# Dealing a two-term combination to three engines instead of one, in an attention plus mixture-of-experts kernel

## The reference

```
scores = x_norm @ Wg.T                      # 8 experts
topk_s, topk_i = top_k(scores, 2)
probs = softmax(topk_s)
y = sum over the 2 chosen experts e of prob_e * (silu(x_norm @ W1[e].T) * (x_norm @ W2[e].T)) @ W3[e].T
out = x + y
```

## Time and profile before

| what | us |
|---|---|
| median of 3 runs (lowest, highest) | 553.78 (552.27, 553.94) |
| the profiled execution | 550.32 |
| its span, first to last instruction | 548.5 |

### The profile page before, as it was taken

How to read it: one execution, slowest core, us unless ns; L and a number is a source line. 1 busy time by engine, 2 the same in 40 slices (tenths; PEclk the granted TensorE clock), 3 DMA queues, 4 the chain that set the end, 5 groups by cost and what they waited for, 6 DMA issues and landing times. The chain is left out here.

```text
span 548.5 us, 21635 instructions
## 1 busy us (share of the span) xinstructions
PE 483.5 (88%) x7711; PEld 369.8 (67%) x7711; DVE 418.0 (76%) x1285; ACT 327.8 (60%) x849; POOL 354.4 (65%) x562
## 2 busy tenths in 40 slices
PE   2789999999999999999999987789999999998730
PEld 2556666766666666767666554659999999987720
DVE  6548899998989899999999876757745554559836
ACT  2365767667676767677676753655556655655420
POOL 5766788888888888888888743303556555565430
PEclk9789999999999999999999998659999999999985
DMA  5101322541222123222110122132344434368948
GB/s 105 37 20 33 98 79 58 140 105 58 72 63 76 59 72 116 72 67 62 49 52 31 34 75 76 40 97 78 118 133 128 126 121 132 114 186 274 321 119 285
DMA packets 55287, 54.61 MB, mean 100 GB/s; under 512 B 12933, under 2 KB 50959, under 8 KB 55184
## 3 DMA queue, kind: packets, MB, share of 16 engines
q1 hardware_dynamic: 48704, 36.41, 23.5%
q0 software_dynamic: 6480, 16.82, 8.7%
HBM read 29.70 MB, written 23.90 MB: 98 GB/s over the span
## 5 line engine op out<-in xcount | busy, mean ns | idle before, releaser
L664 POOL DMA_INDIRECT result_rows<-w12a,blk_dest x71 | 70.0, 986 | 93.9 <-ACT w12a L1177 52.3
L631 POOL DMA_INDIRECT routed_rows<-xs,slots x64 | 66.0, 1031 | 19.3 <-issue 16.8
L722 DVE TENSOR_REDUCE negmax<-logit_banks 128x16 f32<-128x1024 f32 x64 | 75.0, 1214 | 1.0 <-PE logit_banks L1254 1.0
L1090 ACT ACTIVATE late<-logit_banks 128x1024 f32<-128x1024 f32 x64 | 62.0, 1021 | 16.7 <-PE logit_banks L1281 16.7
L994 DVE TENSOR_TENSOR gated<-act_h,logit_banks 128x176 f32<-128x176 f32 x71 | 23.9, 337 | 53.3 <-ACT act_h L1182 44.8
L638 POOL TENSOR_TENSOR mid<-rope_a,mid 128x512 f32<-128x512 f32 x32 | 41.2, 1287 | 31.9 <-DVE mid L707 31.9
L729 DVE RECIPROCAL rden<-bank 128x256 f32<-128x256 f32 x32 | 56.0, 1750 | 3.6 <-PE bank L1306 3.4
L1449 PE MATMUL logit_banks<-w_hi,x_hi 128*128 x142 | 48.0, 338 | 9.2 <-DVE x_lo L1005 8.3
L1182 ACT ACTIVATE act_h<-logit_banks 128x176 f32<-128x176 f32 x71 | 22.6, 318 | 52.8 <-PE logit_banks L1449 52.8
L1449 PE MATMUL logit_banks<-w_hi,x_lo 128*128 x142 | 46.5, 327 | 0.0
L1449 PE MATMUL logit_banks<-w_lo,x_hi 128*128 x142 | 46.5, 327 | 0.0
(11 more groups left out here) (218 smaller groups left out, 1349.5 us busy)
## 6 DMA issues: line engine op xcount, KB each, us to landing
xb<-routed_rows SPq DMA_DIRECT2D x71, 128.5 KB, 2.2
w_raw<-result_rows SPq DMA_DIRECT2D x32, 256.0 KB, 4.3
x_sb<-in_x_dram SPq DMA_DIRECT2D x32, 128.0 KB, 2.1
out_dram<-w12b SPq DMA_DIRECT2D x16, 256.0 KB, 4.2
ctx_sb<-in_ctx_dram SPq DMA_DIRECT2D x32, 64.0 KB, 2.0
mid<-mT SPq DMA_DIRECT2D x128, 4.0 KB
routed_rows<-pad_row SPq DMA_DIRECT2D x15, 128.5 KB, 3.3
w_raw<-in_L_ffn_W_dram SPq DMA_DIRECT2D x2, 704.0 KB
```

The costliest lines, as they stand in the source:

```text
L631: nc.gpsimd.indirect_dma_start(routed[:, :], bass.IndirectOffsetOnAxis(ap=slots[:, t.slot(TR), k:k + 1], axis=0), xs[:, t.slot(TR), k, :], ...
L664: nc.gpsimd.indirect_dma_start(results[:, :], bass.IndirectOffsetOnAxis(ap=blk_dest[:, b.slot(RB):b.slot(RB) + 1], axis=0), y_sb[:, b.slot ...
L722: V.tensor_reduce(negmax[:, t.par, 16 * half:16 * half + 16], ps_s[:, 1024 * half:1024 * half + 1024].rearrange("p (h k) -> p h k", k=N), ...
L1090: S.activation(pT[:, 1024 * half:1024 * half + 1024], ps_s[:, 1024 * half:1024 * half + 1024], ACT.Exp, scale=SCALE).then_inc(exp_done, 1)
```

## The change

The combination of a unit is dealt to three engines. ACT does `y_half = p1 * y1` (`weigh(v)`, two activations) at the end of the unit's block, POOL adds the residual in place (`add_rows(v)`, one operation of 128x512) at the end of the same block in its own program, and DVE does `o = p2 * y2 + y_half` (two operations) one block later. `y_half` has two buffers, used in turn; the second one is the memory of `x_sb`, which the attention no longer needs. `store_unit` stands one block later in SP's order. Units 10 to 15 go through the same three steps behind the blocks.

```diff
-        y_half = rope_a[:].rearrange("p (a d) -> p a d", a=2)
+        y_half = [rope_a[:].rearrange("p (a d) -> p a d", a=2), x_sb[:]]
...
-                for v in unit_at(c - RB - 2):
+                for v in unit_at(c - RB - 3):
                     store_unit(v)
...
+            def add_rows(v):
+                pool.wait_ge(share_done, 2 * v + 2)
+                nc.gpsimd.tensor_tensor(y_half[v % 2], y_half[v % 2], xres[:, 2 * v:2 * v + 2, :], ALU.add)\
+                    .then_inc(half_done, 1)
+
             def ffn_body(do, b):
                 do(take_dest, b)
                 do(store_block, b.plus(-2))
+                for v in unit_at(b.c):
+                    add_rows(v)
 
             blocks(pool, ffn_body, 2)
+            for v in range(T1 // 2, UNITS):
+                add_rows(v)
...
             def combine(v):
                 u = v % 4
-                dve.wait_ge(y_back[u], 32 * (v // 4) + 32)
-                wait_past(dve, o_done, 2 * v)
-                for a in range(2):
-                    t = 2 * v + a
-                    V.scalar_tensor_tensor(y_half[:, a], y_in[:, u, 0, a], wtop[:, 0, t:t + 1], xres[:, t, :],
-                                           ALU.mult, ALU.add).then_inc(half_done, 1)
+                dve.wait_ge(half_done, v + 1)
                 wait_past(dve, o_stored[u], 16 * (v // 4))
                 for a in range(2):
                     t = 2 * v + a
-                    dve.wait_ge(half_done, t + 1)
-                    V.scalar_tensor_tensor(o_sb[:, u, a], y_in[:, u, 1, a], wtop[:, 1, t:t + 1], y_half[:, a],
+                    V.scalar_tensor_tensor(o_sb[:, u, a], y_in[:, u, 1, a], wtop[:, 1, t:t + 1], y_half[v % 2][:, a],
                                            ALU.mult, ALU.add).then_inc(o_done, 1)
...
-                for v in unit_at(b.c):
+                for v in unit_at(b.c - 1):
                     combine(v)
...
+                for v in unit_at(b.c):
+                    weigh(v)
+
+            def weigh(v):
+                u = v % 4
+                act.wait_ge(wtop_done, 3)
+                act.wait_ge(y_back[u], 32 * (v // 4) + 32)
+                wait_past(act, o_done, 2 * v - 2)
+                for a in range(2):
+                    t = 2 * v + a
+                    S.activation(y_half[v % 2][:, a], y_in[:, u, 0, a], ACT.Copy, scale=wtop[:, 0, t:t + 1])\
+                        .then_inc(share_done, 1)
...
             blocks(act, ffn_body, 2)
+            for v in range(T1 // 2, UNITS):
+                weigh(v)
```

More of the change, by code:

```diff
@@ L319, in xattn_ffn_kernel @@
         y_back = [sem(f"y_back{n}") for n in range(4)]
-        half_done, o_done = sem("half_done"), sem("o_done")
+        share_done, half_done, o_done = sem("share_done"), sem("half_done"), sem("o_done")
         o_stored = [sem(f"o_stored{n}") for n in range(4)]
@@ L543, in _ @@
                 move_units(c)
-            for c in range(NBLK, NBLK + RB + 4):
+            for c in range(NBLK, NBLK + RB + 5):
                 move_units(c)
```

## The result

The changed kernel takes 563.5 us (median of 4 runs, 562.2 to 565.58) against 553.02 (4 runs, 550.62 to 553.94) for the kernel before: ratio 1.02 [1.0149, 1.025], 10.5 us slower. The sign was forecast, the size was not: 558.0 with a range to 561.0. The profiled execution took 562.41 us, its span 560.5.

The account below looks back on a forecast made before the run. PE was taken to set the pace up to 487.5 us, then lost time in the mixed stretch; the tail is a chain through units 11 and 15. Tail +3.2 and stretch +1.0 on 553.78 gave 558.0 us, range 553.6 to 561.0.

Parts of the forecast that it names:

- The prices of the three operations: Per unit: ACT's two activations 0.90 us, POOL's add of 128x512 1.29, DVE's remaining pair 0.88.
- The loop: Mixed stretch: landing, ACT, POOL's add, `take_dest`, SP's next loads take 8.74 us per three blocks, which PE does in 5.94.
- The gain per awaited unit: Mixed stretch: with the same landing, PE's next block comes 0.46 us earlier per unit that waits for its landing.
- The tail: After the blocks: units 11 and 15 lie in series, each ending 1.58 us later; +3.2 us, bounds 2.2 to 3.9.
- the last load should take clearly less than 4.45: Tail: a stated sign that the prediction is wrong; it kept the transfer of unit 15 at 4.45 us.
- The wait of `weigh` on the unit two before: Blocks and tail: the second buffer's new wait was costed at nothing, being over when it comes.
- the mixed stretch: Blocks with units 0 to 9 between them: gain and loss together +1.0 us, bounds -4.6 to +3.5.
- POOL's short time: Mixed stretch: a block with a unit costs POOL 2.47 us against 1.98; 0.8 taken of a loss of 1.2.
- the upper bound: Mixed stretch: +3.5 us if the register load again takes 2.8 where now little of it shows.
- POOL is slower: Rival: beside DVE's two-input operations each add takes up to 0.88 us more; +7.0, 560.8 us; chance 0.13.
- The gain pays for the tail: Rival: SP's loads come no later, 3.2 us return in the mixed stretch, time stays at 553.8; chance 0.22.
- Faster: Rival: all 4.6 us return in the mixed stretch and block 66's idle time shrinks; -3.3, 550.5 us; chance 0.07.

Follow-up runs that it names:

- e4: Changed kernel, with POOL taking destinations two blocks earlier in its program; ratio 1.0005 [0.9903, 1.0107] to the kernel before.
- e5: Kernel before, with POOL taking destinations two blocks earlier in its program and nothing else; ratio 0.9921 [0.9874, 0.9968], 544.85 us beside 549.1.
- first profile: Changed kernel unaltered, its first execution in the profiler; 562.41 us.
- e3: Kernel before, with one tiny POOL memset (128x2) behind a wait for the last combination; ratio 1.0088 [1.0019, 1.0157].
- second profile: Changed kernel unaltered, a second execution in the profiler; 562.3 us beside 549.92 for the kernel before.
- e10: Changed kernel with destinations two blocks earlier, no register load before block 66, DVE's pair one block later, three buffers, units 10 to 15 on DVE alone; ratio 0.9974.
- e9: Kernel before, with destinations taken two blocks earlier and no register load ahead of block 66; ratio 0.9968 [0.9928, 1.0008].
- e7: Kernel before, with four POOL adds of 128x512 in the tail, at the landings of units 10 to 13, results unread; 553.25 us beside 549.1.

## Why the prediction was wrong

*Right.* The prices of the three operations (0.91, 1.26 and, alone, 0.88 for 0.90, 1.29, 0.88). The loop: `take_dest` of block 59 came 2.3 later (2.4 forecast), the load of unit 3 left 1.9 later, and e4 and e5 show that this order of POOL's work sets SP's loads. The gain per awaited unit too: from the start of a unit's first operation to the next block's `gate` it was 1.59 us (unit 1), and from the start of `weigh` it is 1.14 for units 0 to 5 of the changed kernel, 0.45 less for the 0.46 forecast.

*Right in size, by luck.* The tail measured +3.2 to +3.6 for +3.2, on another path. I let unit 11's pair meet no add, as DVE would have run out of work. It met unit 12's add (1.88 for 0.88), and in the first profile the load of unit 15 left 3.1 us later from the tail's start, not 1.58. Then its transfer took 3.2 us where I had kept 4.45, which gave 1.2 back; why was not examined. That the last load should take clearly less than 4.45 was a sign of being wrong, and it came. The wait of `weigh` on the unit two before, which "is over in both stages when it comes", held unit 13, and unit 15 by 0.2 us.

*A term that is missing: +3.1.* The sum ended with the last store. POOL now works until the tail's last add, and its closing DRAIN, which ended unseen in the kernel before, ends last. e3 shows such a cost, 4.1 us there, without anything else of the change.

*A term mis-sized: the mixed stretch, +1.0 forecast.* In the second profile it measured +3.5, in the first +7.9. Behind block 70's gate it is +1.5 and +1.6 (5.82 and 6.00 for 4.37): POOL's short time, which I priced at 0.8 in all, comes on the last block's path, where no later block makes it up. DVE waited 1.13 us there for unit 9's add, and `h_lo` stood behind that pair. Dealt and mended it still costs 1.9 (e10), and with the combination on DVE it is absent in every run. The other +2.0 of the second profile lies between the gates of blocks 56 and 70 (39.12 for 37.07). There the late loads are one cause: I had priced the loop at +1.6 at block 64 and at 0.25 from block 67 on, because the kernel before already loses 2.81 at block 66, and walked only through units 1, 3 and 5. The gate of block 64 came 3.2 and 3.4 us later than before in the two profiles, that of block 67 5.6 and 1.6. DVE's wait for the adds is likely another (e4 beside e5, above). How the 2.0 divide between the two was not shown. The remaining 4.4 of the first profile come with the idle 4.16 us before block 66, the 4.34 of register load and the 0.50 clock behind it; what made them stays open. I had named the register load for the upper bound, +3.5 (1.0 and 2.8 would be 3.8), and left it out of the sum.

*The rivals.* "POOL is slower" had the nearest time (560.8) and the contention, but the wrong way round: POOL's add nearly keeps its price and DVE pays. So its nearness is luck as well; it had no closing DRAIN. "The gain pays for the tail" fell at its own point of decision: aligned to block 56's gate, the load of unit 3 left 1.9 us late. "Faster" fell with it.

Together, by the second profile: 3.2 (tail) + 3.1 (end) + 1.5 (behind the last gate) + 2.0 (between the gates) = 9.8 beside the 10.5 between the medians. By the first profile it would be 14.5. So the step that failed first is the sum's end at the last store, and the second is the mixed stretch.

## What to carry to other kernels

An engine that hands out destinations or issues stores delays all who wait for these as soon as it gets arithmetic in between; move such duties ahead first. Here that alone, two blocks earlier, was worth 0.9921 [0.9874, 0.9968] without the change (0.9968 [0.9928, 1.0008] in e9, which holds it too). Compare such an edit with and without the change, as it may mend what the kernel before has lost as well. Before an idle engine gets the program's last work, read in the profile how long its closing instructions take and what covers them now. And a pair of operations dealt to two engines is worth its row only if the two don't run at once on the same memory: look for a row where both are busy.

## What the runs showed of the hardware

- POOL's closing DRAIN ended 6.37 to 6.39 us after POOL's last operation in all 16 profiles, be it a store, an add or a memset of 0.10 us (e3); SP's took 7 ns, DVE's 0.80 in e3.
- An operation on DVE with two inputs in SBUF that meets a POOL add of 128x512 is held until the add ends: in e7 it ended 0.28 us after the add each time, and its pair took about 1 us more per add. The add took 1.26 there, and 1.40 in the changed kernel where it began while a DVE operation was under way.
- The load of expert numbers on PE ahead of block 66 took 1.06 to 4.34 us in the 11 profiles that have it. That the transfers beside it cause this was not settled.
- After 4.16 us without a matmul the granted clock was 0.50, and after the 2.81 us before block 66 in the kernel before it was 1.00 (window of 513.5 to 517). The length of the idle time alone doesn't decide it: in e4 the clock was 0.57 in the 3.9 us behind an idle time of 1.78 (window of 507.88 to 511.80).
